# Decoder kernel, second phase: third encoder product in three pieces, turns moved next to turns, two query heads finished a step later

## Chip, core and metric

The kernel runs on one core of a Trainium2 chip. Such a core has five engines with queues of their own, each of which works through its instructions in program order: PE (TensorE: matrix products, and the transposes that this document calls turns), DVE (VectorE), ACT (ScalarE), POOL (GpSimd) and SP (SyncE, which here only issues DMAs). PE's weight loads are listed apart as PEld. Engines wait for each other through semaphores. The metric is the device time of one execution in microseconds.

## The reference

All shapes are for 16 sequences of 512 tokens by 512 features, in float32. A decoder layer of three parts runs over them, each on the layer-normed x and added back to x:

```python
x = x + attn(layernorm(x))            # linear attention with 16 heads and a 3-tap convolution
x = x + xattn(layernorm(x), ctx, mask)
x = x + ffn(layernorm(x))             # gated recurrence over the 16 sequences, then a tanh layer
# xattn, the part that the change touches:
xn, mn = rmsnorm(x, scale), rmsnorm(ctx, scale)
q = rope(xn @ q_w) * 128 ** -0.5      # 4 query heads of width 128
k, v = rope(mn @ k_w), mn @ v_w       # one key/value head
probs = softmax(where(mask, q @ k.T, -2.38e38))
out = (probs @ v) @ out_w
```

## The kernel before

Every float32 product is made from two parts of each operand, a high one (rounded to fp32r) and a low one (the remainder), as three matmuls into one PSUM bank (`product`, L130, L131, L132). So nearly every product needs a `..._high` copy on ACT and a `..._low` subtraction on DVE or POOL before it, and each bank of PSUM is read twice before it is free.

The program has phases, one for each part of the layer; the second (`phase_b`, tiles named `b_...`) is the one changed. It is a pipeline of three stages over the 16 sequences. In step s it works on three sequences at once: `new` (number s: turns of the normed tokens, keys, values and queries), `old` (s - 1: logits, softmax, turned probabilities, encoder products) and `fin` (s - 2: the last encoder product, the output projection and the residual). Steps run from 0 to 17; a step with all three stages is called full here, and the steps that have a `new` and an `old` are 1 to 15. Each step is written as 16 slots, j = 0 to 15, one for each tile of 128 queries of one of the 4 heads, and each engine's code has its own list of what it does in which slot. No planner decides anything: the order is that of the code.

What happens to tile j of `old`, once in every slot:

- PE `logits` (L130 to L132, `b_l`) two slots ahead; DVE `masked` (L1398, L1399) adds the mask and finds the maximum; ACT `exp` (L1257) makes the exponentials and their sum; DVE `one_over` (L1388); POOL `normalise` (L1213).
- PE `turn_p` (L1580, `b_t<-ident,b_soft`, four transposes) stands last in PE's slot. It waits for `p_lo` of the tile before, since there is one bank `b_t`, and for `normalise`.
- ACT `p_high` (L1266) and then DVE `p_low` (L1407) stand first in the next slot. So from one `turn_p` to the next there is always a way over ACT and DVE.

Between `logits` and `turn_p` of a slot stands what else PE has to do: `keys_values` in slots 0 and 2, `encode(fin, 3)` in 1, `turn_x` and `out` in 3 to 6, `encode(old, 0)` in 7, `turn_keys` and `queries(0)` in 8, `queries(1)` in 9, `encode(old, 1)` in 10, `queries(2)` and `(3)` in 11 and 12, `turn_memory` (eight transposes of the next sequence's context) in 13 and 14, and `encode(old, 2)` in 15. In step 0, `a_last_output` in slots 3 to 6 is the last projection of the first phase.

A query head is finished by ACT `query_swap` (L1301, L1302), DVE `query_cos` (L1453), POOL `query_sin` (L1217), DVE `query_add` (L1458, both inputs and the output in `b_rope`), ACT `query_high` (L1308) and POOL `query_low` (L1221). Heads 2 and 3 are first used by the logits of slots 6 and 10 of the next step. `x_power` (POOL, L344 to L1037) computes the scale of the next sequence's norm from `norm_variance` (DVE, L332 to L336); `norm_apply` (DVE, L350) uses it. Four banks `b_n` go round among all the other products (`Rota`), each with the event that frees it.

## Time and profile before

| | us |
|---|---|
| time, median of 3 runs | 3249.42 (3244.93 to 3250.12) |
| the profiled execution: its own time | 3249.04 |
| its span | 3247.3 |
| around the span | 1.7 |
| PE busy | 3177.4 |
| DVE busy | 1799.3 |
| ACT busy | 1351.7 |
| POOL busy | 1019.7 |
| second phase, about | 908 to 1963 |
| mean of one `p_high`, `exp` (ACT) | 0.593, 0.724 |
| mean of one `p_low`, `masked` (DVE) | 0.687, 0.685 |
| mean of one `normalise` (POOL) | 1.579 |

The profile is of one execution. A row of a timeline gives the start, the duration, the engine, the line and what is written and read; `[0.47 <-DVE b_p_lo L1407]` says that the engine had been idle so long and what released it. Matmuls are pipelined, so their durations overlap: what one costs is the distance between two starts. The idle time in brackets is taken between the modelled ends and so can be less than what PE lost; where it matters, starts are compared.

### The profile page before, as it was taken

To read this page: it belongs to the slowest core of one execution; us is meant where nothing else is said; L and a number is where in the kernel's file an instruction comes from. 1 tells how busy PE (TensorE), PEld (TensorE's weight loads), DVE (VectorE), ACT (ScalarE), POOL (GpSimd) and SP (SyncE) were. 2 spreads that over 40 slices of the span, in tenths; PEclk is the share of its full clock that TensorE was granted. 3 is DMA by queue.
4 is the path that set the end of the run, shared out by engine and by line. 5 is a ranking of instruction groups with operands and counts; after the bars stand their busy time and mean duration, and the time that the engine had idled before them with its cause. 6 is when DMAs were issued, how large, how long until landed. Compare 5 with 4: busy or idle time off the path is not lost.

```text
span 3247.3 us, 41066 instructions
## 1 busy us (share of the span) xinstructions
PE 3177.4 (98%) x15748; PEld 2656.4 (82%) x15748; DVE 1799.3 (55%) x3797; ACT 1351.7 (42%) x2575; POOL 1019.7 (31%) x838
## 2 busy tenths in 40 slices
PE   7999999999989999999999989999999999999998
PEld 6888888888867888888888878888888888888887
DVE  5666666757577777777777766222222322222564
ACT  4444444344446666676666653111121112111233
POOL 1323323232346666666566550000000000000243
PEclk9999999999999999999999999999999999999999
DMA  3112121212231211211222131000000000100343
GB/s 107 40 45 73 39 78 39 78 40 78 69 109 41 92 67 54 92 64 57 79 66 67 53 117 65 14 14 14 14 27 14 14 14 14 56 1 14 118 168 130
DMA packets 102866, 189.29 MB, mean 58 GB/s; under 512 B 6928, under 2 KB 13072, under 8 KB 102672
## 3 DMA queue, kind: packets, MB, share of 16 engines
q1 hardware_dynamic: 102672, 186.68, 17.1%
q8 instruction: 125, 2.05, 0.3%
q14 instruction: 69, 0.57, 0.1%
HBM read 136.33 MB, written 50.33 MB: 57 GB/s over the span
## 4 chain that ended last, share of the span: by engine, by line
PE 91%; DVE 4%; ACT 2%; issue 2%; POOL 1%; DMA 0%; POOLq 0%; DVEq 0%; ACTq 0%
PE c_p L132 10%; PE c_p L130 10%; PE c_p L131 10%; PE a_p L130 6%; PE a_p L131 6%; PE a_p L132 6%; PE b_n L132 4%; PE b_n L130 4%; PE b_n L131 4%; PE b_t L1580 3%; PE a_r L132 2%; PE a_r L130 2%; PE a_r L131 2%; PE d_p L132 2%; PE d_p L130 2%
## 5 line engine op out<-in xcount | busy, mean ns | idle before, releaser
L1213 POOL TENSOR_SCALAR b_soft<-b_soft,b_one_in_sum 128x512 f32<-128x512 f32 x256 | 404.3, 1579 | 304.3 <-DVE b_one_in_sum L1388 304.3
L1780 ACT ACTIVATE c_gate<-c_p,c_bias 128x512 f32<-128x512 f32 x180 | 124.2, 690 | 731.9 <-PE c_p L132 731.9
L1814 DVE TENSOR_TENSOR c_gate<-c_gate,c_gate 128x512 f32<-128x512 f32 x64 | 44.3, 692 | 536.2 <-ACT c_gate L1780 536.2
L344 POOL TENSOR_TENSOR kept_scale<-c_ln_ve,minus_half 128x4 f32<-128x4 f32 x16 | 16.1, 1009 | 897.8 <-DVE c_ln_ve L336 897.8
L1407 DVE TENSOR_TENSOR b_p_lo<-b_t,b_p_hi 128x512 fp32r<-128x512 f32 x256 | 175.9, 687 | 203.8 <-ACT b_p_hi L1266 201.0
L1257 ACT ACTIVATE b_soft<-b_soft,b_minus_top 128x512 f32<-128x512 f32 x256 | 185.3, 724 | 214.9 <-DVE b_minus_top L1399 210.2
L570 ACT ACTIVATE a_elu<-a_p 128x512 f32<-128x512 f32 x128 | 76.6, 598 | 331.9 <-PE a_p L132 285.1
L1266 ACT ACTIVATE b_p_hi<-b_t 128x512 fp32r<-128x512 f32 x256 | 151.8, 593 | 95.5 <-PE b_t L1580 95.3
L1580 PE MATMUL b_t<-ident,b_soft 128*128 128x128 f32 x1024 | 158.2, 277 | 24.5 <-DVE b_p_lo L1407 21.2
L1998 POOL TENSOR_TENSOR d_x<-d_x,d_y 128x512 f32<-128x512 f32 x64 | 82.8, 1295 | 295.0 <-ACT d_y L2010 295.0
L1399 DVE CUSTOM_DVE_ANT_0 b_soft<-b_l,b_mask_row 128x512 f32<-128x512 f32 x256 | 175.4, 685 | 0.0
L1580 PEld LDWEIGHTS b_t<-ident,b_soft 128*128 128x128 f32 x1024 | 123.0, 142 | 61.2 <-DVE b_p_lo L1407 38.3
L538 POOL TENSOR_TENSOR a_att<-a_att,a_local 128x512 f32<-128x512 f32 x64 | 94.1, 1478 | 139.6 <-DVE a_att L751 139.6
L344 POOL TENSOR_TENSOR a_ln_sc<-a_ln_ve,minus_half 128x4 f32<-128x4 f32 x16 | 16.3, 1017 | 377.1 <-DVE a_ln_ve L336 377.1
L130 PE MATMUL b_l<-b_k_hi,b_q_hi 128*128 128x512 f32 x256 | 122.7, 479 | 0.0
L702 DVE SCALAR_TENSOR_TENSOR a_elu<-a_p,a_elu 128x512 f32<-128x512 f32 x64 | 44.3, 692 | 137.7 <-ACT a_elu L572 137.7
L547 POOL TENSOR_TENSOR a_q_lo<-a_elu,a_q_hi 128x512 fp32r<-128x512 f32 x64 | 81.2, 1280 | 109.7 <-ACT a_q_hi L576 109.7
L1816 DVE TENSOR_TENSOR c_gate<-c_gate,c_c_f 128x512 f32<-128x512 f32 x64 | 44.3, 692 | 123.0 <-ACT c_gate L1780 123.0
L130 PE MATMUL a_p<-a_Wk_hi,a_xT_hi 128*128 128x512 f32 x256 | 101.0, 395 | 5.1 <-DVE a_local L798 5.1
L130 PE MATMUL b_n<-b_ow_hi,b_enc_hi 128*128 128x512 f32 x256 | 105.4, 412 | 0.0
L130 PE MATMUL a_r<-a_Wp_hi,a_z_hi 128*128 128x512 f32 x256 | 103.8, 406 | 0.0
L132 PE MATMUL b_l<-b_k_hi,b_q_lo 128*128 128x512 f32 x256 | 101.9, 398 | 0.0
(311 smaller groups left out, 10019.6 us busy)
## 6 DMA issues: line engine op xcount, KB each, us to landing
a_x<-in_x SPq DMA_DIRECT2D x16, 1024.0 KB, 8.1
a_res<-in_x SPq DMA_DIRECT2D x16, 1024.0 KB, 6.7
x<-a_res SPq DMA_DIRECT2D x16, 1024.0 KB, 5.2
b_mem<-in_ctx SPq DMA_DIRECT2D x16, 1024.0 KB, 5.3
b_x<-x SPq DMA_DIRECT2D x16, 1024.0 KB, 5.6
b_res<-x SPq DMA_DIRECT2D x16, 1024.0 KB, 5.6
x<-b_res SPq DMA_DIRECT2D x16, 1024.0 KB, 4.3
c_x<-x SPq DMA_DIRECT2D x16, 1024.0 KB, 5.6
```

The lines of the kernel that those rows point to most:

```text
L130: pe.matmul(out, stationary.high, moving.high, start=first, stop=False)
L131: pe.matmul(out, stationary.high, moving.low, start=False, stop=False)
L132: return pe.matmul(out, stationary.low, moving.high, start=False, stop=last)
L538: pool.tensor_tensor(att[c % 2][:, :], att[c % 2][:, :], local[old.par][:, c, :], ALU.add).then_inc(z_f.sem, z_f.unit)
L1213: pool.tensor_scalar(soft[:, at, :], soft[:, at, :], one_in_sum[:, at:at + 1], None, ALU.mult).then_inc(p_norm.sem, p_norm.unit)
L1257: act.activation(soft[:, at, :], soft[:, at, :], ACT.Exp, bias=minus_top[:, at:at + 1], scale=-1.0, accum_out=row_sum[:, at:at + 1]).then_ ...
L1266: act.activation(p[h % 2].high[:, :, t * P:(t + 1) * P], pT_bank[:, :].rearrange("p (i s) -> p i s", i=T), ACT.Copy).then_inc(p_hi.sem, p_ ...
L1399: dve.tensor_tensor_reduce(out=soft[:, at, :], in0=logit_banks[j % 2][:, :], in1=mask_row[b % 2][:, :], scale=-1.0, scalar=3e38, op0=ALU.a ...
L1407: dve.tensor_tensor(part.low, pT_bank[:, :].rearrange("p (i s) -> p i s", i=T), part.high_f32(), ALU.subtract).then_inc(p_lo.sem, p_lo.unit)
L1580: mm = pe.transpose(pT_bank[:, i * P:(i + 1) * P], soft[:, tile(old.b, j), i * P:(i + 1) * P], self.ident[:, :])
L1780: act.activation(gate[j % 2][i][:, :], gating.banks[(3 * j + i) % 6][:, :], ACT.Tanh if g == "c" else ACT.Sigmoid, bias=added[:, i, j:j + ...
L1998: pool.tensor_tensor(x[old.par][:, t, :], x[old.par][:, t, :], y[:, t % 2, :], ALU.add).then_inc(out_sb.sem, out_sb.unit)
```

## The change

In the second phase:

- `encode(old, 2)`, twelve matmuls in slot 15, becomes three pieces: three matmuls in slot 13, three in slot 14 and six in slot 15, each behind `logits` and ahead of `turn_memory`.
- `turn_x` in slots 3 to 6 stands behind `out` (and behind `a_last_output` in step 0), so right ahead of `turn_p`. `turn_keys` goes from slot 8 to the end of slot 7, ahead of `turn_p`. ACT's `tokens_high` goes from slots 3 to 6, behind `exp`, to slots 4 to 7, ahead of `exp`.
- Where a further sequence follows, `query_add`, `query_high` and `query_low` of head 2 go from slots 14, 15 and 15 to slots 0, 1 and 2 of the next step, and those of head 3 from 14, 15 and 0 to 4, 5 and 6.
- `norm_variance` goes from slot 14 to slot 13 on DVE.

```diff
                             normalise(old.b, j + 1)
                         if new and j == J - 1:
                             normalise(new.b, 0)
-                        if old and j == 0:
+                        if old and new and j == 2:
+                            query_low(old.b, 2)
+                        if old and new and j == 6:
+                            query_low(old.b, 3)
+                        if old and not new and j == 0:
                             query_low(old.b, 3)
                         if j == 7 and following(new, B):
                             mem_power(pool, new.b + 1)
...
                             if j == 13:
                                 query_sin(new.b, 2)
                                 query_sin(new.b, 3)
-                            if j == 15:
+                            if j == 15 and not following(new, B):
                                 query_low(new.b, 2)
                         if j == 14 and following(new, B):
                             x_power(pool, new.b + 1)
...
                             if j == 2:
                                 enc_high(fin.b, 3)
                         if old:
+                            if new and j == 1:
+                                query_high(old.b, 2)
+                            if new and j == 5:
+                                query_high(old.b, 3)
                             if j == 8:
                                 enc_high(old.b, 0)
                             if j == 11:
...
                                 query_high(new.b, 1)
                             if j == 13:
                                 query_swap(3)
-                            if j == 15:
+                            if j == 15 and not after:
                                 query_high(new.b, 2)
                                 query_high(new.b, 3)
+                        if new and 4 <= j <= 7:
+                            tokens_high(j - 4)
                         if after and j >= 14:
                             memory_high(act, s, after, 2 * (j - 14))
                             memory_high(act, s, after, 2 * (j - 14) + 1)
...
                             exp(old.b, j + 2)
                         if new and j >= J - 2:
                             exp(new.b, j - J + 2)
-                        if new and 3 <= j <= 6:
-                            tokens_high(j - 3)
                         if s == 1 and 3 <= j <= 6:
                             output_weight_high(act, j - 3)
                         if after:
...
                             if j == 2:
                                 enc_low(fin.b, 3)
                         if old:
+                            if new and j == 0:
+                                query_add(old.b, 2)
+                            if new and j == 4:
+                                query_add(old.b, 3)
                             if j == 8:
                                 enc_low(old.b, 0)
                             if j == 11:
...
                                 query_cos(2)
                             if j == 13:
                                 query_cos(3)
-                            if j == 14:
+                            if j == 14 and not after:
                                 query_add(new.b, 2)
                                 query_add(new.b, 3)
                         if fin and 4 <= j <= 7:
...
                         if after:
                             if 9 <= j <= 12:
                                 self.norm_tile(dve, N, after, x, j - 9)
+                            if j == 13:
+                                self.norm_variance(dve, N, after)
                             if j == 14:
-                                self.norm_variance(dve, N, after)
                                 memory_low(dve, s, after, 0)
                                 memory_low(dve, s, after, 1)
                             if j == 15:
...
                             mm = pe.transpose(pT_bank[:, i * P:(i + 1) * P], soft[:, tile(old.b, j), i * P:(i + 1) * P], self.ident[:, :])
                         mm.then_inc(pT_ps.sem, pT_ps.unit)
 
-                    def encode(item, h):
-                        if free := earlier(enc_lo, item.b, h, 1):
-                            pe.wait_ge(*free)
-                        pe.wait_ge(v_lo.sem, v_lo.upto(item.b))
-                        pe.wait_ge(p_lo.sem, p_lo.upto(item.b, h * T + T - 1))
-                        for i in range(T):
+                    def encode(item, h, keys=range(T)):
+                        if keys[0] == 0:
+                            if free := earlier(enc_lo, item.b, h, 1):
+                                pe.wait_ge(*free)
+                            pe.wait_ge(v_lo.sem, v_lo.upto(item.b))
+                            pe.wait_ge(p_lo.sem, p_lo.upto(item.b, h * T + T - 1))
+                        for i in keys:
                             mm = product(pe, enc_bank[:, :], v[item.par][:, i, :], p[h % 2][:, i, :], i == 0, i == T - 1)
-                        mm.then_inc(enc_ps.sem, enc_ps.unit)
+                        if keys[-1] == T - 1:
+                            mm.then_inc(enc_ps.sem, enc_ps.unit)
 
                     def keys_values(g):
                         bank = bank_of(KV + g)
...
                         if new and j == 2:
                             keys_values(1)
                         if 3 <= j <= 6:
-                            if new:
-                                turn_x(j - 3)
                             if fin:
                                 out(j - 3)
                             if s == 0:
                                 self.a_last_output(pe, j - 3)
+                            if new:
+                                turn_x(j - 3)
                         if old and j == 7:
                             encode(old, 0)
+                        if new and j == 7:
+                            turn_keys()
                         if new and j == 8:
-                            turn_keys()
                             queries(0)
                         if new and j == 9:
                             queries(1)
...
                             queries(2)
                         if new and j == 12:
                             queries(3)
+                        if old and j >= 13:
+                            encode(old, 2, ((0,), (1,), (2, 3))[j - 13])
                         if following(new, B) and j in (13, 14):
                             turn_memory(pe, s, new.b + 1, 2 * (j - 13))
                             turn_memory(pe, s, new.b + 1, 2 * (j - 13) + 1)
-                        if old and j == 15:
-                            encode(old, 2)
                         for i, c, bank in gate_weight(s, j) or ():
                             if (i, c) in ((0, 0), (0, 1), (4, 0), (4, 1)):
                                 if freed := turns.freed(s, 2 * c):
```

On PE, the end of slot 13 and the start of slot 14 of a full step, before (`b_l` are logits, `b_mem` the context being turned, `b_soft` the probabilities, `b_e` the encoder product):

```order
L132 MATMUL b_l<-b_k_hi,b_q_lo 128x512
L356 MATMUL b_n<-ident,b_mem 128x128 x8
L1580 MATMUL b_t<-ident,b_soft 128x128 x4
L130 MATMUL b_l<-b_k_hi,b_q_hi 128x512
L131 MATMUL b_l<-b_k_lo,b_q_hi 128x512
L132 MATMUL b_l<-b_k_hi,b_q_lo 128x512
```

The same place now:

```order
L132 MATMUL b_l<-b_k_hi,b_q_lo 128x512
L130 MATMUL b_e<-b_p_hi,b_v_hi 128x512
L131 MATMUL b_e<-b_p_lo,b_v_hi 128x512
L132 MATMUL b_e<-b_p_hi,b_v_lo 128x512
L356 MATMUL b_n<-ident,b_mem 128x128 x8
L1593 MATMUL b_t<-ident,b_soft 128x128 x4
L130 MATMUL b_l<-b_k_hi,b_q_hi 128x512
L131 MATMUL b_l<-b_k_lo,b_q_hi 128x512
L132 MATMUL b_l<-b_k_hi,b_q_lo 128x512
```

Three matmuls of the encoder product have come between the logits and the turned context; slot 14 has three more in the same place, and slot 15 keeps six.

On DVE, slots 14 and 15 of a full step, before (`b_rope` is the query addition, `b_ln_...` the variance, `b_nT_lo` the context's low part, `b_p_lo` the low part of the turned probabilities):

```order
L1407 TENSOR_TENSOR b_p_lo<-b_t,b_p_hi 128x4x128
L1398 MEMSET b_carrier 128x1
L1399 ISA b_soft,b_minus_top<-b_l,b_mask_row_208 128x512
L1399 ISA b_minus_top 128x1
L1458 TENSOR_TENSOR b_rope<-b_rope 128x512 x2
L332 MEMSET b_ln_carrier 128x1
L334 BN_AGGR b_ln_mv<-b_ln_st 128x2 x4
L336 TENSOR_SCALAR b_ln_ve<-b_ln_mv 128x4
L1143 TENSOR_TENSOR b_nT_lo<-b_n,b_nT_hi 128x512 x2
L1388 RECIPROCAL b_one_in_sum<-b_row_sum 128x1
L1407 TENSOR_TENSOR b_p_lo<-b_t,b_p_hi 128x4x128
```

The same place now, from the variance on, which stands in slot 13:

```order
L332 MEMSET b_ln_carrier 128x1
L334 BN_AGGR b_ln_mv<-b_ln_st 128x2 x4
L336 TENSOR_SCALAR b_ln_ve<-b_ln_mv 128x4
L1396 RECIPROCAL b_one_in_sum<-b_row_sum 128x1
L1415 TENSOR_TENSOR b_p_lo<-b_t,b_p_hi 128x4x128
L1406 MEMSET b_carrier 128x1
L1407 ISA b_soft,b_minus_top<-b_l,b_mask_row_208 128x512
L1407 ISA b_minus_top 128x1
L1143 TENSOR_TENSOR b_nT_lo<-b_n,b_nT_hi 128x512 x2
L1396 RECIPROCAL b_one_in_sum<-b_row_sum 128x1
L1415 TENSOR_TENSOR b_p_lo<-b_t,b_p_hi 128x4x128
```

Between `masked` of slot 14 and `p_low` of slot 15 only the context's low parts and the reciprocal are left; both additions are gone and the variance stands a slot earlier.

On PE, slots 2 and 3 of step 0, before (`b_kvw` the key and value product, `a_r` the last projection of the first phase):

```order
L132 MATMUL b_n<-b_kvw_hi,b_nT_lo 128x256
L356 MATMUL b_n<-ident,b_x 128x128 x4
L130 MATMUL a_r<-a_Wp_hi,a_z_hi 128x512
L131 MATMUL a_r<-a_Wp_lo,a_z_hi 128x512
L132 MATMUL a_r<-a_Wp_hi,a_z_lo 128x512
```

The same place now:

```order
L132 MATMUL b_n<-b_kvw_hi,b_nT_lo 128x256
L130 MATMUL a_r<-a_Wp_hi,a_z_hi 128x512
L131 MATMUL a_r<-a_Wp_lo,a_z_hi 128x512
L132 MATMUL a_r<-a_Wp_hi,a_z_lo 128x512
L130 MATMUL a_r<-a_Wp_hi,a_z_hi 128x512
```

The turn of the tokens has gone behind the twelve matmuls of `a_last_output`.

## Rows read from the trace of the kernel before

**Rows 1.** The page: busy time, share of the span and instructions by engine.
```profile
PE 3177.4 (98%) x15748; PEld 2656.4 (82%) x15748; DVE 1799.3 (55%) x3797; ACT 1351.7 (42%) x2575; POOL 1019.7 (31%) x838
```

**Rows 2.** Stretches: length, busy time by engine, granted TensorE clock, DMA share, GB/s.
```profile
930.00:940.00 10.00, 7.00 (x24) 5.60 (x24) 7.28 (x15) 1.84 (x5) 2.34 (x2) 0.66 0.01 2
...
1886.00:1897.00 11.00, 8.96 (x39) 6.84 (x38) 6.45 (x20) 7.01 (x16) 10.41 (x8) 0.84 0.00 0
...
1052.00:1868.00 816.00, 808.79 (x4474) 679.66 (x4473) 614.65 (x1706) 531.25 (x1136) 518.13 (x432) 1.00 0.21 69
```

**Rows 3.** Timeline of PE, slots 13 to 0 of a full step.
```profile
1330.83 0.66 PE L1580 MATMUL b_t<-ident,b_soft 128*128 128x128 f32 x4
...
1332.02 1.03 PE L356 MATMUL b_n<-ident,b_mem 128*128 128x128 f32 x8
1333.52 0.66 PE L1580 MATMUL b_t<-ident,b_soft 128*128 128x128 f32 x4 [0.47 <-DVE b_p_lo L1407]
...
1337.22 0.39 PE L132 MATMUL b_e<-b_p_hi,b_v_lo 128*128 128x512 f32 x1
1337.71 0.66 PE L1580 MATMUL b_t<-ident,b_soft 128*128 128x128 f32 x4
...
1341.78 0.60 PE L1580 MATMUL b_t<-ident,b_soft 128*128 128x128 f32 x4
```

**Rows 4.** Waits from 1052 to 1868: total, times, longest.
```profile
PEld b_t L1580 <- DVE b_p_lo L1407: 15.8, 26, 0.7
...
PEld b_n L356 <- issue: 4.3, 13, 0.3
```

**Rows 5.** DVE, ACT, POOL beside rows 3; last, the query addition's minimum/median/maximum ns.
```profile
1332.78 0.69 DVE L1407 TENSOR_TENSOR b_p_lo<-b_t,b_p_hi 128x512 fp32r<-128x512 f32 x1 [0.33 <-ACT b_p_hi L1266]
...
1334.00 1.30 DVE L1458 TENSOR_TENSOR b_rope<-b_rope 128x512 f32<-128x512 f32 x2
...
1336.99 0.67 DVE L1407 TENSOR_TENSOR b_p_lo<-b_t,b_p_hi 128x512 fp32r<-128x512 f32 x1
...
1335.32 1.14 ACT L1308 ACTIVATE b_q_hi<-b_rope 128x512 fp32r<-128x512 f32 x2
...
1335.89 1.04 POOL L344 TENSOR_TENSOR b_ln_sc<-b_ln_ve,minus_half 128x4 f32<-128x4 f32 x1 [0.85 <-DVE b_ln_ve L336]
...
1339.10 1.57 POOL L1213 TENSOR_SCALAR b_soft<-b_soft,b_one_in_sum 128x512 f32<-128x512 f32 x1
...
L1458 DVE TENSOR_TENSOR b_rope<-b_rope x64: 668/882/1694, 956.6 to 1892.6; 128x512 f32<-128x512 f32 x64
```

**Rows 6.** Timeline of PE, step 0, slots 2 to 8.
```profile
929.95 0.28 PE L132 MATMUL b_n<-b_kvw_hi,b_nT_lo 128*128 128x256 f32 x1
933.23 1.09 PE L356 MATMUL b_n<-ident,b_x 128*128 128x128 f32 x4 [3.00 <-DVE b_x L350]
...
939.11 0.60 PE L356 MATMUL b_n<-ident,b_x 128*128 128x128 f32 x4
...
948.69 0.60 PE L1624 MATMUL b_n<-ident,b_k_f 128*128 128x128 f32 x4
```

**Rows 7.** Step 1: PE, slots 0 and 1, then ACT, slot 4.
```profile
971.48 0.66 PE L1580 MATMUL b_t<-ident,b_soft 128*128 128x128 f32 x4 [0.34 <-POOL b_soft L1213]
974.54 0.63 PE L1580 MATMUL b_t<-ident,b_soft 128*128 128x128 f32 x4 [1.71 <-POOL b_soft L1213]
...
985.47 0.72 ACT L1257 ACTIVATE b_soft<-b_soft,b_minus_top 128x512 f32<-128x512 f32 x1 [1.38 <-DVE b_minus_top L1399]
...
986.19 0.57 ACT L1287 ACTIVATE b_nT_hi<-b_n 128x512 fp32r<-128x512 f32 x1
```

**Rows 8.** PE, turns of probabilities in slots 14, 15 (step 15) and 13 (step 16).
```profile
1891.51 1.12 PE L1580 MATMUL b_t<-ident,b_soft 128*128 128x128 f32 x4 [1.32 <-DVE b_p_lo L1407]
...
1896.94 0.27 PE L1580 MATMUL b_t<-ident,b_soft 128*128 128x128 f32 x1
...
1946.14 1.12 PE L1580 MATMUL b_t<-ident,b_soft 128*128 128x128 f32 x4 [1.32 <-DVE b_p_lo L1407]
```

## The prediction

> **What bounds the kernel.** I read the page first: PE is busy 3177.4 of 3247.3 us, no other engine above 1799.3 [rows 1]. The reader is to see that PE is the limit, so that the change can only bring back time in which PE stands still or runs at a low clock. It adds and removes no instruction, but moves some. The stretches come next [rows 2]: over steps 2 to 14 (1052 to 1868) PE is busy 808.8 of 816 us at full clock, while in steps 0 and 15 there are stretches with a granted clock of 0.66 and 0.84 of full speed. So there are two things to win: about a microsecond in each full step, and holes at the two ends of the phase. PE's timeline shows where the microsecond is [rows 3], the waits how regular it is [rows 4], and the other engines beside it what PE waits for [rows 5]. Rows 6 to 8 are the same for the ends.
>
> **A. Slots 13 to 15, 14 steps (1 to 14).** The eight turns of `b_mem` in slot 14 start at 1332.02, last 1.03 to the end of the pipeline and start about 0.11 apart, so that PE is free again 0.87 later, at 1332.89; yet the probabilities' turn starts at 1333.52: 0.63 lost. The encoder product's last matmul starts at 1337.22 and frees PE 0.23 later, yet the next turn starts at 1337.71: 0.26. A turn that had to wait also takes 0.66 instead of 0.60, its weight load not having been pulled ahead, three times in these slots [rows 3]. Together 0.63 + 0.26 + 3 x 0.06 = 1.07 us a step. The weight loads' own wait says the same from another side: 15.8 us in 26 times over 13 steps, 1.2 a step [rows 4].
>
> After the change slots 13 and 14 hold each 1.19 us from turn to context (1330.83 to 1332.02), three matmuls (12 take from 1334.71, which is 1333.52 + 1.19, to 1337.45, so 0.69 for three) and 0.87: 2.75 us. The turns then stand at about 1331.5 (13), 1334.25 (14) and, with six matmuls left, 1.19 + 1.37 later, 1336.8 (15). What is late next? Each turn waits for the low part of the one before. Before, the way from turn 13 (1330.83) to the end of that low part (1332.78 + 0.69) was 2.64 us [rows 3, 5], with ACT busy with an `exp` at its start. With the same way, turn 14 could go at 1334.15 and turn 15 at 1336.9, against 1334.25 and 1336.8: met, or missed by 0.1. Lining up the mean durations of the table by each engine's own order, I get a little room: low part 13 ends at 1333.6; `masked` and `exp` of the next sequence's first tile hold ACT until 1334.9, so low part 14 ends at 1336.3; then DVE does two parts of the context and `masked` (to 1338.1), ACT `exp` and `p_high`, and low part 15 ends at 1340.2. PE reaches turn 0 at 1336.8 + 4.07 - 0.06 - 0.1 = 1340.7, the old distance [rows 3] without the late weight load and a little rounding. This works only since the additions (1.30) are gone from DVE and the two high copies (1.14) from ACT there; before, `p_low` came at 1336.99 behind them, for a turn at 1337.71 [rows 5]. POOL has `x_power` between `normalise` 15 and 0; it idled 0.85 until 1335.89 for the variance, which is now early, so it starts at 1335.04, and `normalise` 0, which starts 3.21 later and takes 1.57, ends at 1339.8 instead of 1340.7 [rows 5]. So all of it comes back: 14 x 1.07 = **15.0 us**; bounds 0 (another chain just as long behind it) and 15.
>
> **B. Turns next to turns, slots 3 to 8.** Turns cost their 0.11 us each whether another group stands before them or not, so that merging as such is worth nothing; but `turn_x` had waited 0.3 us on the weight load in slot 3 for the normalised x, 13 times in 13 steps [rows 4], of which I take a third as PE's, the rest lying under running matmuls, and `out` covers that now. 14 x 0.1 = **1.4 us**; bounds 0 and 14 x 0.3 = 4.2.
>
> The moved query work: in slot 0 DVE gets an addition of 0.67, in slot 1 ACT a copy of 0.57, in slot 2 POOL 1.29, and the same in 4, 5, 6. Queued behind the addition are `norm_apply` and the low part that turn 1 needs; that one is ready about 1343.6, for a turn at 1344.6. In slots 4 to 6 DVE and ACT each idle over 1.3 us. I cost it at 0; if the cover went, it would be 0.65 to 1.3 us a step. The logits of slots 6 and 10 need their heads only after slots 2 and 6.
>
> **C. Step 0.** PE ends the value product at 929.95 + 0.12 and stands until 933.23 for the first normalised x, then runs `turn_x` and twelve matmuls at half clock: 5.88 us to 939.11, where the next three rounds take (948.69 - 939.11) / 3 = 3.19 each [rows 6]. Granted clock 0.66 in this stretch, after the idle [rows 2]. Now the twelve matmuls, which wait for nothing of x, fill 2.75 of the 3.16 us at full clock; turn at 933.23, 0.44, then three rounds of 3.19: 943.24 instead of 948.69, **5.4 us**. Bounds: 2.7 (the fill alone, clock low all the same) and 5.6.
>
> **D. From step 0 to 1.** Turn 0 at 971.48 and turn 1 at 974.54 wait for POOL, which has `x_power` and two `query_low` around the `normalise`s [rows 7]: 0.34 and 1.71 us of idle, and ahead of them the variance had waited for DVE's two additions. With the variance ahead of the mask, `x_power` follows `query_sin` directly, and both `query_low` are gone from between. The waits of 2.05 are the measure; some of turn 1's stays, for its low part takes over. **1.9 us**; bounds 0 and 3.
>
> **E. Step 1, slots 4 to 6.** No output product fills PE; each slot is a ring over ACT and DVE. ACT idles 1.38 us before `exp` while DVE works, and does `tokens_high` after it, with 0.48 us to what follows [rows 7]. The copy now falls into the 1.38. 3 x 0.48 = **1.4 us**; bounds 0 and 1.9.
>
> **F. The end.** In step 15 turn 14 waits 1.32 us and comes at half clock, turn 15 at 1896.94, 5.43 later [rows 8]; granted clock 0.84 [rows 2]. Six matmuls leave slot 15 (1.37), and six fill holes ahead of it; if that keeps the clock up, as much again. But the ring over ACT and DVE allows no turn 15 before about 1894, and turn 0 of step 16 follows by its own ring: 2.2 us in all. In step 16 the wait of 1.32 [rows 8] takes up three matmuls and the slot after it three more: 1.4. Sum **3.6 us**; bounds 1.4 and 5.
>
> Sum: 15.0 + 1.4 + 5.4 + 1.9 + 1.4 + 3.6 = 28.7. The profiled execution took 3249.0 (span 3247.3 and 1.7 around it), 0.4 below the median of the runs. 3249.0 - 28.7 = 3220.3; I say 3220.5. What follows the phase is PE-bound too, so the time is not given back.
>
> **Rivals.**
> 1. The pieces fill the holes of slots 13 and 14, but the way over ACT and DVE holds turn 15 or turn 0 where it was. For it: the margins above are only 0.4 to 0.7 us. Against: both engines lose over 1.1 us of work there. Then A is 0 to 7: with the rest (13.7) 3249 - 13.7 - 3.5 = 3232.
> 2. DVE and POOL hinder each other in slots 0 to 3. The addition takes 668 ns at least, 882 in the middle and 1694 at most [rows 5], so something lengthens it; in slots 0 and 1 POOL runs two `normalise`s in a row. If an addition takes 1.69 and `norm_apply` behind it is stretched as well, turn 1's margin of 1.0 us is overrun by 0.3 to 0.7 a step, 14 x 0.5 = 7: 3227.5. The Trainium skill (SBUF — State Buffer, "Who interferes with whom") says that a DVE instruction with two SBUF inputs shares its second read path with POOL, and that whoever starts first blocks the other for a whole instruction. The spread in rows 5 agrees. By that rule alone the addition could wait for a whole `normalise`, the case that this rival takes from the longest row.
> 3. Slower than before: the chain from turn 14 over ACT and DVE to turn 0 (just short of the 8.26 us from 1333.52 to 1341.78 before) does not shorten, since the context's turns that it also waits for come 1.4 us later. Started at 1334.25 instead of 1333.52 it would put turn 0 at most 0.7 after its old place, and an addition stretched to 1.69 in slot 0, with 0.8 of it not covered, makes 1.5 a step: 14 x 1.5 = 21 lost against 13.7 from B to F, 3256. It decides from 13.7 / 14 = 1.0 us a step on. Against: copies and additions of 2.4 us have left this chain.
> 4. The ends stay as they were (C to F at their lower bounds, 2.7 + 1.4 = 4.1): 3249 - 15 - 1.4 - 4.1 = 3228.5.
>
> **Chances.** Forecast with all terms near their values 0.60; rival 1 0.14, rival 2 0.10, rival 4 0.10, rival 3 0.03, and 0.03 that several fail together and nothing measurable is left. Below the forecast lie the upper bounds: B 2.8 more, D, E, F some 3 more, 3214. The range takes in rivals 1, 2 and 4: 3213 to 3234. A difference of 0.2% (6.5 us) is about what a measurement of this kernel can tell from none; faster by more than that 0.93, within it 0.04, slower 0.03.
>
> **What would show it.** In the new profile: no idle before the turns of probabilities in slots 14 and 15 of full steps, and these at distances of 2.75, 2.75 and 2.55 us; a full step shorter by 1.1 to 1.2 us; `a_r` matmuls directly behind 929.95 with one turn of x at 933.2 and `turn_keys` near 943; POOL's `x_power` without the 0.85 us idle; slots 4 to 6 of step 1 at 3.8 us where they had 4.3; clock above 0.9 in the stretches of rows 2. Wrong it would be if a turn in slots 15, 0 or 1 now shows an idle from `b_p_lo`, if the queries of step 0 start later than 944, or if a later wait eats what the ends give.

## The result, and the profile after

The changed kernel takes **3220.57 us** (median of 4 runs, 3219.72 to 3220.98) against 3248.06 before (3244.93 to 3250.12): ratio 0.9916, 95% interval 0.9899 to 0.9933. The profiled execution took 3220.54, its span 3218.8 us, 28.5 less than before. The forecast was 3220.5. The sum was right; four of its six terms (A, B, E and F) were mis-sized, and they cancelled.

The page of the changed kernel, busy time by engine, answers to [rows 1]. PE's work is the same, and what it lost is idle and half clock:

```profile
PE 3165.3 (98%) x15748; PEld 2655.7 (83%) x15748; DVE 1822.6 (57%) x3797; ACT 1350.2 (42%) x2575; POOL 1017.4 (32%) x838
```

The stretches of [rows 2] in the changed kernel. The granted clock in step 0 is 1.00 where it was 0.66, and PE has work in all but 0.4 of these 10 us; the full steps (1028 to 1841) show PE busy throughout. The last row is step 15, where 0.84 stood:

```profile
930.00:940.00 10.00, 9.63 (x49) 7.83 (x48) 8.99 (x18) 3.41 (x9) 2.79 (x2) 1.00 0.01 2
1028.00:1841.00 813.00, 813.00 (x4533) 692.96 (x4533) 647.60 (x1732) 538.35 (x1154) 522.28 (x437) 1.00 0.19 69
1860.00:1871.00 11.00, 10.19 (x55) 7.60 (x53) 7.35 (x21) 8.41 (x18) 9.98 (x8) 1.00 0.00 0
```

DVE is the surprise on the page: 23 us more busy time (1822.6 for 1799.3) for the same 3797 instructions. Something on DVE has become longer (it will be two things, L336 with 14 us and a pair of L350 with 13, while the rest became a little less). The timeline of PE answers to [rows 3]; turns 12, 13, 14, 15 and 0:

```profile
1312.95 0.60 PE L1593 MATMUL b_t<-ident,b_soft 128*128 128x128 f32 x4
...
1315.66 0.60 PE L1593 MATMUL b_t<-ident,b_soft 128*128 128x128 f32 x4
...
1318.36 0.66 PE L1593 MATMUL b_t<-ident,b_soft 128*128 128x128 f32 x4
...
1321.03 0.66 PE L1593 MATMUL b_t<-ident,b_soft 128*128 128x128 f32 x4
...
1325.09 0.60 PE L1593 MATMUL b_t<-ident,b_soft 128*128 128x128 f32 x4
```

The distances are 2.71, 2.70, 2.67 and 4.06 us. The first two are those of the forecast within 0.05, but turn 15 should have come 2.55 after turn 14, and turns 14 and 15 take 0.66 instead of 0.60, as the turns did before that had to wait. The waits over the full steps (total, times, longest), for the 15.8 us of [rows 4], confirm it, and the waits on the turn of x are gone:

```profile
PEld b_t L1593 <- DVE b_p_lo L1415: 4.8, 13, 0.4
```

DVE and POOL beside these turns show why. The variance's last instruction (L336, which adds 1e-5 to 128x4 numbers) has moved from slot 14 to slot 13:

```profile
1316.48 1.17 DVE L336 TENSOR_SCALAR b_ln_ve<-b_ln_mv 128x4 f32<-128x4 f32 x1
...
1317.63 0.67 DVE L1415 TENSOR_TENSOR b_p_lo<-b_t,b_p_hi 128x512 fp32r<-128x512 f32 x1
```
```profile
1315.08 2.54 POOL L1217 TENSOR_TENSOR b_rope<-b_rope,b_sin_q 128x512 f32<-128x512 f32 x2
```

It lasts 1.17 us. POOL's two multiplications by the sine take 1.3 each, the second from 1316.32 on; L336 starts 0.16 behind that and ends with it (1317.65 and 1317.62). It is so in all 14 steps from 1 to 14: L336 ends 0.03 us behind POOL's instruction each time. The low part of turn 13 stands behind it and starts at 1317.63.

Step 0, answering to [rows 6]: the key and value product ends, `a_last_output` follows at once, one turn of x waits 0.37, and `turn_keys` stands at 943.71 (forecast 943.2; before 948.69):

```profile
930.28 0.28 PE L132 MATMUL b_n<-b_kvw_hi,b_nT_lo 128*128 128x256 f32 x1
930.40 0.40 PE L130 MATMUL a_r<-a_Wp_hi,a_z_hi 128*128 128x512 f32 x1
...
933.68 0.63 PE L356 MATMUL b_n<-ident,b_x 128*128 128x128 f32 x4 [0.37 <-DVE b_x L350]
...
943.71 0.60 PE L1639 MATMUL b_n<-ident,b_k_f 128*128 128x128 f32 x4
```

A ledger over the phase, from the starts of the same turns before and after: steps 0 to 1 give 7.7 us (C and D), slots 3 to 8 of step 1 give 3.0 (E), slots 13 to 15 of steps 1 to 14 give 0.80 each (11.2, A), slots 3 to 8 of steps 2 to 15 some 0.265 each (3.7, B), the end 2.9 (F). That is the whole 28.5. A full step went from 62.00 to 60.93 us.

### The profile page after: what moved, and what is told of

It is laid out like the page before. It is cut to its first block, busy times and chain, and to the rows that moved or that the text cites. A ratio compares the mean times of both kernels' runs of the same rounds, so it can differ in the third digit from the quotient of the medians.

```text
span 3218.8 us, 41066 instructions
## 1 busy us (share of the span) xinstructions
PE 3165.3 (98%) x15748; PEld 2655.7 (83%) x15748; DVE 1822.6 (57%) x3797; ACT 1350.2 (42%) x2575; POOL 1017.4 (32%) x838
## 4 chain that ended last, share of the span: by engine, by line
PE 94%; DVE 2%; ACT 1%; POOL 1%; issue 1%; DMA 0%; POOLq 0%; ACTq 0%; DVEq 0%
PE c_p L132 11%; PE c_p L130 11%; PE c_p L131 11%; PE a_p L130 6%; PE a_p L131 6%; PE a_p L132 6%; PE b_n L130 4%; PE b_n L132 4%; PE b_n L131 4%; PE b_t L1593 3%; PE a_r L132 2%; PE a_r L130 2%; PE a_r L131 2%; PE b_l L132 2%; PE b_l L130 2%; PE b_l L131 2%
## 5 line engine op out<-in xcount | busy, mean ns | idle before, releaser
L130 PE MATMUL b_e<-b_p_hi,b_v_hi 128*128 128x512 f32 x256 | 101.0, 395 | 0.8 <-DVE b_enc_lo L1420 0.8
```

The source lines that it names most:

```text
L130: pe.matmul(out, stationary.high, moving.high, start=first, stop=False)
```

## The experiments

Ten further kernels were run, and the changed one and e7 a second time. The kernel before ran beside each set, at 3248.4 to 3248.8 us. The diffs show the lines that matter and leave out the rest of each edit. In full steps, the distances of the turns tell the kernels apart:

| kernel | 12 to 13 | 13 to 14 | 14 to 15 | 15 to 0 | full step | time |
|---|---|---|---|---|---|---|
| before | 2.01 | 2.69 | 4.19 | 4.07 | 62.00 | 3248.1 |
| changed | 2.71 | 2.70 | 2.67 | 4.06 | 60.93 | 3220.6 |
| split alone (e1) | 2.70 | 2.70 | 3.50 | 4.05 | 62.00 | 3245.4 |
| changed without split (e2) | 2.01 | 3.39 | 3.94 | 4.01 | 62.10 | 3239.0 |
| changed, queries at old places (e3) | 2.71 | 2.69 | 3.68 | 4.06 | 61.93 | 3237.4 |
| changed, turns at old places (e5) | 2.70 | 2.71 | 2.68 | 4.06 | 62.13 | 3245.0 |
| changed, 1e-5 added on POOL (e7) | 2.71 | 2.69 | 2.52 | 4.00 | 60.69 | 3218.2 |

### Which part brings the full step's microsecond

**e1.** Before, with the split and nothing else.

```diff
+ if old and j >= 13:
+     encode(old, 2, ((0,), (1,), (2, 3))[j - 13])
- if old and j == 15:
-     encode(old, 2)
```

> The kernel before with the encoder product of head 2 in three pieces (3, 3 and 6 matmuls in slots 13 to 15) and nothing else. My theory: the pieces alone bring nothing, since the low part that turn 15 waits for stands on DVE behind two query additions (1.30 us), the variance and two low parts of the context, all of which now start 0.7 us later. Turn 15 then comes 0 to 0.3 us later than before in each full step, and only the end of the phase gains 2 to 3 us: 3245 to 3250. Rival: the pieces are what pays and the moved query work only makes room elsewhere; then 14 x 0.8 to 1.07 us come back here: 3233 to 3237.

Measured 3245.35 us (3243.26 to 3247.53), ratio 0.9992 (0.9983 to 1.0001): my theory, and against before no clear gain. Of the 4.2 us between the two profiled executions 3.2 stand at the end of the phase. The holes of slots 13 and 14 are filled, and the time that this won now stands as one wait ahead of turn 15. PE's row, and DVE's, which releases it, behind the two additions (1333.12, 1.29):

```profile
1336.82 0.66 PE L1580 MATMUL b_t<-ident,b_soft 128*128 128x128 f32 x4 [0.82 <-DVE b_p_lo L1407]
```
```profile
1333.12 1.29 DVE L1458 TENSOR_TENSOR b_rope<-b_rope 128x512 f32<-128x512 f32 x2
...
1336.09 0.67 DVE L1407 TENSOR_TENSOR b_p_lo<-b_t,b_p_hi 128x512 fp32r<-128x512 f32 x1
```

**e3.** The changed kernel with additions, high copies and low parts of queries 2 and 3 at their old places.

```diff
- if new and j == 0:
-     query_add(old.b, 2)
- if new and j == 4:
-     query_add(old.b, 3)
- if j == 14 and not after:
+ if j == 14:
      query_add(new.b, 2)
      query_add(new.b, 3)
```

> The changed kernel with the additions, high and low parts of query heads 2 and 3 back in slots 14, 15 and 0. My theory: DVE has 1.2 us more between masked and the low part in slots 14 and 15, so that turn 15 comes 1.0 us later in each full step, and turn 0 of step 1 some 1.5 us later: 3220.5 + 14 + 1.5 = 3236. PE should idle some 1.2 us before turn 15. Rival, that the chain had more room than I worked out: under 3225.

Measured 3237.43 us (3236.89 to 3239.45), ratio 0.9965 (0.9952 to 0.9978), a full step of 61.93. Turn 15 of each full step waits 0.95 for its low part, and the additions stand ahead of that one. What is left of the gain is that of the phase's two ends; term B's 0.265 us a step is there too, but turn 15 now comes so late that it takes most of this back.

**e2.** The changed kernel without the split.

```diff
- if old and j >= 13:
-     encode(old, 2, ((0,), (1,), (2, 3))[j - 13])
+ if old and j == 15:
+     encode(old, 2)
```

> The changed kernel without the split: the twelve matmuls of the third encoder product stand together in slot 15 again, all else as changed. My theory (the low part of turn 13 comes no earlier than 5.3 us after turn 12, because L336 waits on DVE for POOL's two query_sin; with no matmuls between, PE stands there): turn 12 to 13 in 2.0 us, 13 to 14 in 3.3 to 3.4, 14 to 15 in 3.9, 15 to 0 in 4.1, so 1.2 to 1.3 us more a full step than changed (62.15 to 62.25), 3237 to 3241 us. Rival (L336 costs only the 0.26 seen in the changed kernel, the hole is the old 0.63): 0.6 to 0.7 a step, 3229 to 3233 us.

Measured 3238.95 us (3238.34 to 3240.82), ratio 0.9970 (0.9958 to 0.9982), a full step of 62.10 (forecast 62.15 to 62.25). The four distances are the forecast ones within 0.1. PE's turn 14:

```profile
1324.94 0.66 PE L1593 MATMUL b_t<-ident,b_soft 128*128 128x128 f32 x4 [1.17 <-DVE b_p_lo L1415]
```

Without matmuls to put there, the hole in slot 14 is larger than before, since L336 now stands in the way of the low part of turn 13.

**e5.** The changed kernel with `turn_x`, `turn_keys` and `tokens_high` at their old places (the diff shows the first).

```diff
  if 3 <= j <= 6:
+     if new:
+         turn_x(j - 3)
      if fin:
          out(j - 3)
      if s == 0:
          self.a_last_output(pe, j - 3)
-     if new:
-         turn_x(j - 3)
```

> The changed kernel with turn_x, turn_keys and tokens_high at their old places, split and query additions as changed. My theory (terms B, C and E come from this order, and add up): C and the clock 4.3 to 5.4, E 3.0 to 3.3, B 0.25 us in each of 14 steps, 3.4: 3231 to 3234 us, full step 61.15 to 61.2. Rival (they overlap: the ring of step 1 hides what step 0 lost, or B is the ring's): 3226 to 3229 us.

Measured 3245.04 us (3240.86 to 3247.32), ratio 0.9989 (0.9980 to 0.9998). **Both theories failed**: 11 us above mine, with a full step of 62.13. The distances in slots 13 to 15 are those of the changed kernel; 1.06 of the 1.20 us lost in a step stand in slot 3, at PE's first turn of x:

```profile
1349.46 0.63 PE L356 MATMUL b_n<-ident,b_x 128*128 128x128 f32 x4 [0.85 <-DVE b_x L350]
```

The reason is to be seen in the changed kernel itself, in slots 2 and 3. DVE normalises the last two tiles of x (`norm_apply`); POOL has started the moved `query_low` 0.11 us before; PE's turn of x comes late enough, behind `out`. One row of each engine:

```profile
1333.08 1.93 DVE L350 TENSOR_SCALAR b_x<-b_x,b_ln_mv,b_n_scale 128x512 f32<-128x512 f32 x2
```
```profile
1332.97 1.30 POOL L1221 TENSOR_TENSOR b_q_lo<-b_rope,b_q_hi 128x512 fp32r<-128x512 f32 x1
```
```profile
1336.88 0.60 PE L356 MATMUL b_n<-ident,b_x 128*128 128x128 f32 x4
```

Before, the same pair took half as long, with nothing on POOL at that time:

```profile
1349.77 0.99 DVE L350 TENSOR_SCALAR b_x<-b_x,b_ln_mv,b_n_scale 128x512 f32<-128x512 f32 x2
```

So DVE's pair becomes 0.94 us longer when `query_low` stands in slot 2. All of it falls on the first of the two: it takes 1.48 instead of 0.54 and ends 0.29 behind `query_low`, and the second takes its 0.54. e3 has the new order of turns and no `query_low` in slot 2, and there the pair is short:

```profile
1340.59 0.99 DVE L350 TENSOR_SCALAR b_x<-b_x,b_ln_mv,b_n_scale 128x512 f32<-128x512 f32 x2
```

In the changed kernel the logits are through at 1334.14 and the pair ends at 1335.01; a turn of x straight behind the logits would wait those 0.87, as it does in e5 (0.85), and then for its weights. With `out` between, 2.7 us of matmuls cover it. The turn order thus pays for the query move; that is worth 14 x 1.20 = 16.8 us, beside C and E. Of e5's three items it is the turns that count here: with `tokens_high` alone at its old place (e9, below) a full step stays at 60.94.

The three parts of the full step's gain don't add. Each pair of them alone gives a full step of 61.93 to 62.13 against 62.00 before; only all three give 60.93.

### What L336 costs

**e4.** The changed kernel with the whole variance back in slot 14.

```diff
- if j == 13:
-     self.norm_variance(dve, N, after)
  if j == 14:
+     self.norm_variance(dve, N, after)
      memory_low(dve, s, after, 0)
```

> The changed kernel with the variance back in slot 14 on DVE. In the changed kernel the variance's last instruction, 128x4 values (L336), takes 1.17 us instead of 0.17, ends when POOL's two query sines end, and holds the low part before turn 14. Theory A, DVE waits for POOL's instruction to end: here the low part 13 is 0.7 us earlier and turn 14 has no wait (0.08 now), but L336 stands beside POOL's normalise of tile 15, takes about 0.8 us, and turn 15 comes 0.2 us later than now: 3221 to 3225. Theory B, the instruction was slow for another reason of its place in slot 13: L336 takes 0.17 here, the waits in slots 14 and 15 (0.27 us a step) go: 3216 to 3218.

Measured 3218.43 us (3217.23 to 3219.18), ratio 0.9906 (0.9889 to 0.9922), full step 60.70. The time lies next to theory B's 3216 to 3218, not at A's 3221 to 3225, but B's reason is not met, and A's wait is there without its cost. L336 still does not take its 0.17, for it now stands beside POOL's `normalise`, but nothing that PE waits for is behind it. Its minimum, median and maximum in ns over the full steps:

```profile
L336 DVE TENSOR_SCALAR b_ln_ve<-b_ln_mv x13: 620/629/629, 1075.8 to 1804.2; 128x4 f32<-128x4 f32 x13
```

So moving the variance to slot 13 was itself no gain: it costs 0.24 us in each full step, and what it may give back at the first turn of step 1 is 1.2 to 1.6 in all (965.95 here, 964.72 and 964.34 in two executions of the changed kernel).

**e7.** The changed kernel; POOL does the addition at the start of `x_power`, where the variance is needed.

```diff
+ pool.tensor_tensor(N.var_eps[:, :], N.mv[:, :, 1], ln_eps[:, :], ALU.add)
- dve.tensor_scalar(N.var_eps[:, :], mv[:, :, 1], 1e-5, None, ALU.add)
```

> The changed kernel with L336 (adding 1e-5 to the variance) moved from DVE to POOL, at the start of x_power, in the second phase. Theory A (DVE's 128x4 instruction waited for POOL to finish the query sines and so delayed the low parts behind it): low part 13 starts 0.7 us earlier, the waits before turns 14 and 15 (0.08 and 0.18 us a step) go away, 14 x 0.27 = 3.8 us: 3216.5 to 3217.5. POOL's chain gets 0.3 us longer without cost, as turn 0 has 0.9 us of room there. Theory B (these waits come from the length of the ring over ACT and DVE itself): 3220 to 3221, with the waits where they are.

Measured 3218.17 us (3217.00 to 3219.09), ratio 0.9905 (0.9890 to 0.9920), full step 60.69. The span is 3215.3, 3.5 less than in the changed kernel, where theory A said 3.8; the median lies 0.7 above its range. In a later set it took 3219.61 (3218.58 to 3219.80; **e7_again**) and the changed kernel 3221.44 (3220.13 to 3223.53; **after_again**): 1.8 to 2.4 us apart between medians, less than the 14 x 0.24 = 3.4 of the full steps. Steps 0 and 1 vary from execution to execution: the profiled one of e7_again starts its first turn 1.9 us later than that of after_again and loses 1.4 us more in one slot of step 1. Its expectation and that of after_again:

> The changed kernel with the variance's addition of 1e-5 on POOL, once more, as the standard for the next one: 3217 to 3219 us, full step 60.69.

> The changed kernel once more, as the standard for the others of this call: 3220 to 3221.5 us, a full step of 60.93 us, and L336 of the variance (128x4) at 1.16 to 1.18 us in every full step.

The full steps came out so in both (60.69 and 60.94), and the changed kernel's time; e7_again's 3219.61 lies 0.6 above the expected range. The view of waits lists none of PE or of its weight loads in the full steps of e7, and turn 15 comes 2.52 after turn 14, the 2.55 of the forecast.

**e8.** The changed kernel; L336 takes its 1e-5 from an array in SBUF.

```diff
- dve.tensor_scalar(N.var_eps[:, :], mv[:, :, 1], 1e-5, None, ALU.add)
+ dve.tensor_tensor(N.var_eps[:, :], mv[:, :, 1], self.ln_eps[:, :], ALU.add)
```

> The changed kernel with one instruction in another form: the variance's addition of 1e-5 on DVE, 128x4, takes the constant from a second array in SBUF (TENSOR_TENSOR) and not as a number (TENSOR_SCALAR). Theory A (DVE and POOL share a path to SBUF, and an instruction of DVE that wants it waits for the end of what POOL has started; an instruction with two SBUF inputs wants it too): 1.1 to 1.2 us as before, turns 14 and 15 wait 0.08 and 0.18, 3219.5 to 3221.5 us. Theory B (it is the form with one input and a number that waits, the other does not): 0.17 us, step 60.69, 3216.5 to 3218.5 us.

Measured 3220.74 us (3220.33 to 3221.17), ratio 0.9914 (0.9900 to 0.9929): theory A, and full steps of 60.94. The instruction in its new form, over the full steps:

```profile
L337 DVE TENSOR_TENSOR b_ln_ve<-b_ln_mv,b_ln_eps x13: 1159/1160/1160, 1073.1 to 1804.4; 128x4 f32<-128x4 f32 x13
```

The form doesn't matter; both ask for what POOL holds. The Trainium skill (SBUF — State Buffer, "Who interferes with whom") says so for both, the `tensor_scalar` when it runs in a mode with two ports and the `tensor_tensor` with two inputs in SBUF, and that whoever comes second is blocked until the other's instruction ends. The ends in the rows above, 1317.65 and 1317.62, agree. They agree too for the query additions of the kernel before that started beside `query_sin` or `query_low`: all 32 end 0.55 us behind it. For `normalise` they do not. The two additions at 1334.00 in [rows 5] took 1.30 together, hardly more than two of the shortest, with this beside them:

```profile
1333.44 1.59 POOL L1213 TENSOR_SCALAR b_soft<-b_soft,b_one_in_sum 128x512 f32<-128x512 f32 x1
```

All 30 additions that started beside a `normalise` took 0.68 to 0.70, with 0.4 to 1.0 us of it still to go, though L336 beside it does wait for its end (e4). Here the measurement decides; why the two differ was not tried.

### The ends of the phase

**e6.** The changed kernel, with `turn_x` ahead of `a_last_output` in step 0 alone.

```diff
+ if new and s == 0:
+     turn_x(j - 3)
  if s == 0:
      self.a_last_output(pe, j - 3)
- if new:
+ if new and s > 0:
      turn_x(j - 3)
```

> The changed kernel with the old order in step 0 alone: turn_x ahead of a_last_output there. My theory (term C is the fill of PE's wait for the first normalised x and the clock that falls without it): PE stands from 930 to 933 again, the granted clock falls below 0.8 until 940, turn_keys of step 0 comes 4.5 to 5.5 later, total 3225 to 3226.5. Rival (only the fill counts; the clock falls from other causes or comes back at once): 3222.5 to 3223.5 us.

Measured 3225.76 us (3225.41 to 3226.29), ratio 0.9930 (0.9914 to 0.9947). PE stands 3.02 us, the first turn of x takes 1.08, and the stretch shows the clock of before:

```profile
933.15 1.08 PE L356 MATMUL b_n<-ident,b_x 128*128 128x128 f32 x4 [3.02 <-DVE b_x L350]
...
948.63 0.60 PE L1639 MATMUL b_n<-ident,b_k_f 128*128 128x128 f32 x4
```
```profile
930.00:940.00 10.00, 6.98 (x25) 5.64 (x24) 7.26 (x15) 2.54 (x7) 2.26 (x2) 0.66 0.01 2
```

`turn_keys` comes 5.3 us later than in after_again (943.33). Of that, 5.1 reach the end between the two profiled executions and 4.3 between the medians.

**e9.** The changed kernel with the copies of the tokens behind `exp` again.

```diff
- if new and 4 <= j <= 7:
-     tokens_high(j - 4)
  exp(...)
+ if new and 3 <= j <= 6:
+     tokens_high(j - 3)
```

> The changed kernel with the copies of the tokens (ACT, tokens_high) back behind exp in slots 3 to 6, as before. My theory (term E: in step 1 ACT's ring sets the slots 4 to 6; the copy ahead of exp gave about 0.5 us a slot, and what slots 3 to 8 of step 1 gained beyond 1.4 us came from the clock that stays full): slots 3 to 8 of step 1 longer by 1.2 to 1.6, full steps unchanged at 60.93, total 3221.5 to 3222.5. Rival (all 2.7 us came from the place of the copy): 3223 to 3224. Second rival (the copies matter in full steps too): a full step above 61.0, total above 3224.

Measured 3224.74 us (3223.66 to 3225.87), ratio 0.9927 (0.9912 to 0.9942), full steps unchanged. That is 3.3 us more than after_again: 2.2 above my range and 0.7 above the rival's. Two turns of step 1, the wait ahead of them, and the stretch that follows:

```profile
981.45 0.66 PE L1593 MATMUL b_t<-ident,b_soft 128*128 128x128 f32 x4 [1.81 <-DVE b_p_lo L1415]
...
985.74 0.66 PE L1593 MATMUL b_t<-ident,b_soft 128*128 128x128 f32 x4 [2.41 <-DVE b_p_lo L1415]
```
```profile
985.00:990.00 5.00, 4.26 (x14) 3.50 (x15) 3.30 (x10) 2.91 (x7) 3.35 (x5) 0.67 0.56 200
```

The distance is 4.29, against 3.80 in the changed kernel: 3 x 0.49, near the 1.4 of term E. The rest is the clock. The matmuls from 986.7 on run at the lower of the two levels for a while (0.67 granted in the stretch, 0.63 us each for 0.39), and PE loses another 1.6 us in slot 7. In the changed kernel's first profile it stays at 1.00 there.

The longer idles alone don't decide it, though, and a lower clock doesn't always cost. In after_again, with the short distances of 3.81, it was 0.66 from 975 to 980. In e1, with the long ones of 4.29, it was 0.59 from 985 to 990, while PE had waits around it; slot 7 took 4.29 there as well, where before took 5.59 and e9 5.97. What a low clock costs depends on whether it falls among waits or, as in e9, on a slot full of matmuls.

**e10.** e7, and in step 1 alone the copies of the output weight stand four slots later.

```diff
- if s == 1 and 3 <= j <= 6:
-     output_weight_high(act, j - 3)
+ if s == 1 and 7 <= j <= 10:
+     output_weight_high(act, j - 7)
- if s == 1 and 4 <= j <= 7:
-     output_weight_low(dve, j - 4)
+ if s == 1 and 8 <= j <= 11:
+     output_weight_low(dve, j - 8)
```

> The one before, and in step 1 alone the high parts of the output weight (ACT, 0.52 us each) stand in slots 7 to 10 and not 3 to 6, the low parts (DVE) in 8 to 11. My theory (in slots 4 to 6 of step 1 the distance of two turns is a ring over ACT: what stands between exp and p_high adds its own length): 3.80 becomes 3.25 to 3.35 us a slot, 1.5 to 2.2 us less than e7_again, 3215.5 to 3217 us. Rival (DVE's or POOL's part of the ring takes over at once): distances stay above 3.7, same time as e7_again.

Measured 3219.07 us (3218.42 to 3219.30), ratio 0.9907 (0.9891 to 0.9924), beside 3219.61 for e7_again. The distances became 3.29, as my theory said; the time is the rival's, for what they gave is lost again later:

```profile
979.81 0.66 PE L1597 MATMUL b_t<-ident,b_soft 128*128 128x128 f32 x4 [0.81 <-DVE b_p_lo L1419]
...
983.10 0.66 PE L1597 MATMUL b_t<-ident,b_soft 128*128 128x128 f32 x4 [1.41 <-DVE b_p_lo L1419]
```
```profile
1007.67 0.66 PE L1597 MATMUL b_t<-ident,b_soft 128*128 128x128 f32 x4 [0.66 <-DVE b_p_lo L1419]
...
1020.71 0.63 PE L1597 MATMUL b_t<-ident,b_soft 128*128 128x128 f32 x4 [0.79 <-DVE b_p_lo L1419]
```

The first of these late waits has a moved low part ahead of it on DVE (1005.68, 0.68), itself behind a query addition that took 1.74 beside POOL's `query_low`. From turn 11 of step 1 to turn 0 of step 2 it takes 1.9 us longer than in e7, more than the 1.5 gained; the cause of the second wait is open. Another 1.9 us are lost in step 16, where the granted clock was 0.66 from 1910 to 1920 in e10 and 1.00 in both executions of e7. e10's time can't be told from e7's, and e7 is the simpler kernel.

## Why the prediction was right, point by point

**What bounds the kernel.** Right: PE, and the 28.5 us are idle and half clock taken away.

**A, 15.0 forecast, 11.2 measured.** The mechanism was right: the holes fill, and additions and high copies had to leave the way from turn 14 to turn 15 (e1, e3). The step that failed is the sentence "I get a little room: low part 13 ends at 1333.6", which took L336 at its old length when the variance moved a slot forward. By the prediction's own sign, a turn 15 that waits for `b_p_lo`, this part was wrong. There it costs 1.00 us more on DVE, and the low part of turn 13 starts 0.7 later than in e4. Against e7, turn 14 comes 0.01 later, turn 15 another 0.16 and turn 0 another 0.05; a turn of 0.66 for 0.60 is in the last two. e7 gives it back: 0.24 a step, 3.4 us, of which 0.22 and 3.1 in these slots. The other 0.7 of the 3.8 is in the fill: e7's slots 13 to 15 are 1.02 us shorter than those of before, where the sum said 1.07.

**B, 1.4 forecast, 3.7 measured.** The sign and the cause (the turn's weight load in slot 3) were right; I took a third of its 0.33 us a step as PE's, and 0.265 were. But the term hid something larger. "I cost it at 0", on the moved query work, named a cover for turn 1 and the idle time in slots 4 to 6, and none for the turn of x in slot 3. The cover that matters is `out` ahead of the turn of x in slot 3, which the text counted as worth 0.1 a step. The sentence "if the cover went, it would be 0.65 to 1.3 us a step" holds: e5 shows 1.20.

**C and D, 5.4 + 1.9 = 7.3 forecast, 7.7 measured.** `turn_keys` came at 943.71 for 943.24. e6 takes C back: 5.3 us at that place. D's two waits of [rows 7] became 0.48 on POOL and 0.79 on DVE's low part, the one I had named as taking over.

**E, 1.4 forecast, 3.0 in the ledger, 3.3 by e9.** The ring gives 3 x 0.49 as forecast. Missing was the clock: in the kernel before it was 0.52 from 990 to 995, and slot 7 took 5.59 there, 1.3 more than in e1 with the same ring.

**F, 3.6 forecast, 2.9 measured.** Slots 14 and 15 of step 15 gave 2.75, but 0.7 of it is lost again by turn 0 of the next step, whose ring over ACT and DVE is as long as before; step 16 gave 0.85. It could have given 0.6 more: in e6 and e7 the clock stays at 1.00 from 1910 to 1920, where the changed kernel had 0.83.

**Rivals.** Rival 2 came true as a mechanism and not as a time: DVE and POOL do hinder each other, in slot 2 (`norm_apply`, 0.94 longer) and in slot 13 (L336, 1.00 longer). One is covered and the other costs 0.24 us a step; hence 3220.6 and not 3227.5. It had the wrong partner, too: the long query additions of [rows 5] are those beside `query_sin` and `query_low`, while those beside a `normalise` took 0.70 at most (e8), so the two `normalise`s in slots 0 and 1 were no threat to the moved addition, which took 0.68 there. Rival 1 is what e1 and e3 are: turn 15 held by its low part. In the changed kernel only 0.16 of it is left. Rivals 3 and 4 did not happen: turn 0 comes 6.73 after turn 14 (8.26 before), and the ends gave 13.6.

That the sum met the time to 0.1 us is luck: A was 3.8 too high and F 0.7, B and E together 3.9 too low and C and D 0.4. The sum also started from the profiled execution's 3249.0; between the medians of before and after the gain is 27.5 us, not 28.5.

## What to carry to other kernels

When an instruction is moved on DVE, look at what POOL runs at its new place and not only at what stands in its own queue: 128x4 numbers can cost more than 128x512 (1.17 us against 0.68) if POOL has started first, and the table of mean durations of before doesn't show it. A part of a change that seems worth nothing (here the order of a turn and a product) may be what covers the price of another part; take it out of the whole change before you call it idle, since putting it alone into the kernel before would not show it. And hand a tiny operation to the engine that consumes it: here that removed both the collision and a crossing between engines.

## What the runs showed of the hardware

- L336, 128x4: 0.17 us with POOL quiet (e1), 0.63 beside the rest of a `normalise` (e4), 1.17 beside the second of two multiplications (changed; 1.16 in e2), 1.16 with two inputs (e8). The same 128x4 addition on POOL takes 0.20 (e7; 0.21 in e7_again).
- Beside POOL's `query_low`, the low part (one input from PSUM, one from SBUF) keeps its 0.69 us; the normalisation with numbers per partition (L350) goes from 0.54 to 1.48, ending 0.29 behind it, and the addition of two arrays from SBUF from 0.68 to as much as 1.74 (e10), 0.55 behind it in the kernel before. Beside POOL's `normalise` that addition keeps its 0.68 to 0.70.
- The granted clock in step 1: with turns at distances of 4.29 us and idles of up to 2.5 ahead of them it fell (0.67 from 985 to 990 in e9, 0.59 there in e1, 0.52 from 990 to 995 before). At 3.80 with idles of 1.3 to 2.0 it stayed at 1.00 in one execution of the changed kernel and was 0.66 from 975 to 980 in the other; e7 had 0.50 from 980 to 985 and e6, with its step 0 at the lower level, 0.50 from 985 to 990. What decides it between these was not tried.
